# Windowed attention on one core: row scores in one block over four banks, row and column scores of a group in one step

## The reference, cut to what matters

```python
xs = jnp.roll(_gn(x), (-3, -3), axis=(-2, -1))
qkv = jnp.einsum('bchw,oc->bohw', xs, w_qkv) + b_qkv[None, :, None, None]
# -> q, k, v of shape (B, Hn, Wn, HEADS, 49, 16), 16 x 16 windows in an image
scores = jnp.einsum('bxyhqd,bxyhkd->bxyhqk', q, k) / np.sqrt(16)
out = jnp.einsum('bxyhqk,bxyhkd->bxyhqd', jax.nn.softmax(scores, axis=-1), v)
return x + roll_back(out)
```

## Time and profile before

| | |
|---|---|
| median of 3 runs | 966.29 us |
| profiled execution, whole | 967.17 us |
| profiled execution, span on the core | 965.3 us |
| PE busy | 897.0 us (93%), 46595 matmuls |
| PE weight loads busy | 724.3 us (75%) |
| DVE busy | 738.2 us (76%) |
| ACT busy | 656.9 us (68%) |
| POOL busy | 597.7 us (62%) |
| TensorE clock granted, mean | 0.986 of 2.4 GHz |
| HBM traffic | 53 GB/s |

### The profile page before, as it was taken

The page is one execution under the profiler, slowest core; times in us unless marked ns, Lnnn a source line. Parts: engine busy times, 40 slices in busy tenths (PEclk is TensorE's granted clock), DMA queues, the critical chain, the costliest instruction groups (busy, mean ns, idle before and its releaser), DMA issues.

```text
span 965.3 us, 104413 instructions
## 1 busy us (share of the span) xinstructions
PE 897.0 (93%) x46595; PEld 724.3 (75%) x46595; DVE 738.2 (76%) x1404; ACT 656.9 (68%) x1297; POOL 597.7 (62%) x1067
## 2 busy tenths in 40 slices
PE   0479999999999999999999999999999999999984
PEld 0258888887788888888778888888778888888863
DVE  6667787877878787878878787878877777777762
ACT  1346777776677777777677777777677777777752
POOL 1335666666566767676576767676666767676741
PEclk9999999999999999999999999999999999999996
DMA  9401112112112211221121000000000000000011
GB/s 372 170 4 51 50 67 67 51 49 67 51 49 67 67 53 47 67 67 54 46 67 50 17 33 33 33 17 33 34 17 33 33 33 17 33 33 33 17 36 37
DMA packets 29920, 51.96 MB, mean 54 GB/s; under 512 B 3650, under 2 KB 28868, under 8 KB 29764
## 3 DMA queue, kind: packets, MB, share of 16 engines
q1 hardware_dynamic: 29892, 51.59, 15.1%
HBM read 25.89 MB, written 25.69 MB: 53 GB/s over the span
## 4 chain that ended last, share of the span: by engine, by line
PE 86%; DVE 8%; issue 4%; POOL 1%; ACT 1%; DMA 0%; POOLq 0%; SPq 0%; DVEq 0%; ACTq 0%
PE psum L733 16%; PE psum L785 12%; PE psum L753 11%; PE psum L771 10%; PE psum L717 8%; PE psum L705 8%; PE psum L698 7%; PE psum L797 4%; PE psum L760 3%; PE psum L713 3%; PE psum L740 2%; DVE neg_max L574 2%; DVE stats L494 2%; DVE q_halves L559 1%; DVE mixed L599 1%
## 5 line engine op out<-in xcount | busy, mean ns | idle before, releaser
L374 ACT ACTIVATE probs_t<-psum,exp_scale 128x800 f32<-128x800 f32 x256 | 223.6, 925 | 177.8 <-PE psum L760 177.8
L574 DVE TENSOR_REDUCE neg_max<-psum 100x16 f32<-100x784 f32 x256 | 249.5, 974 | 43.1 <-PE psum L733 18.3
L293 POOL TENSOR_SCALAR neg_halves<-neg_max 100x32 bf16<-100x32 f32 x128 | 60.5, 473 | 289.9 <-DVE neg_max L574 289.9
L733 PEld LDWEIGHTS psum<-k_hi,q_masks 32*128 32x128 f16 x8192 | 174.7, 91 | 47.6 <-issue 46.4
L733 PE MATMUL psum<-k_hi,q_masks 32*128 32x49 f16 x8192 | 197.4, 179 | 4.5 <-issue 2.7
L733 PE MATMUL psum<-k_lo,q_masks 32*128 32x49 f16 x4096 | 182.2, 179 | 0.0
L733 PEld LDWEIGHTS psum<-k_lo,q_masks 32*128 32x128 f16 x4096 | 160.5, 91 | 0.0
L306 POOL TENSOR_TENSOR stage<-mixed,image 128x343 f32 (+7 forms) x256 | 144.7, 586 | 10.7 <-DVE mixed L599 7.2
L351 ACT ACTIVATE xn<-image,shift_c,rstd_c 128x21 f32 (+6 forms) x256 | 132.5, 575 | 8.0 <-DVE shift_c L554 6.1
L753 PE MATMUL psum<-q_masks,k_hi 32*64 32x100 f16 x8192 | 129.1, 219 | 6.1 <-issue 3.5
L785 PE MATMUL psum<-probs_t,v_rows 64*32 64x100 f32 x8192 | 132.1, 254 | 1.7 <-issue 1.7
(11 more groups left out here) (120 smaller groups left out, 1867.8 us busy)
## 6 DMA issues: line engine op xcount, KB each, us to landing
out_dram<-stage SPq DMA_DIRECT2D x64, 224.0 KB, 2.1
out_dram<-stage SPq DMA_DIRECT2D x64, 168.0 KB, 1.9
image<-in_x_dram SPq DMA_DIRECT2D x32, 224.0 KB, 2.6
image<-in_x_dram SPq DMA_DIRECT2D x1, 6104.0 KB, 27.6
image<-in_x_dram SPq DMA_DIRECT2D x34, 168.0 KB, 2.5
image<-in_x_dram SPq DMA_DIRECT2D x6, 896.0 KB, 9.8
image<-in_x_dram SPq DMA_DIRECT2D x1, 728.0 KB, 14.5
w_nat<-in_L_conv_w_qkv_dram SPq DMA_DIRECT2D x1, 192.0 KB, 2.5
```

The source lines that it names most:

```text
L374: nc.scalar.activation(probs_t[:, 2 * u:2 * u + 2, :, :].rearrange("p h a q -> p h (a q)"), psum[:, COL_BANKS[u], 0:PAIRS * ROWS2], ACT.Ex ...
L574: nc.vector.tensor_reduce(neg_max[:, par, 2 * j:2 * j + 2, :], psum[0:ROWS2, ROW_BANKS, 0:GT] .rearrange("p h (w k) -> p h w k", k=TOK), A ...
L733: last = nc.tensor.matmul(psum[:, ROW_BANKS.start + h - 2 * j, w * TOK:(w + 1) * TOK], q_masks[rows, par, low + w * ROWS2:low + w * ROWS2 ...
```

## The change

The four banks 0 to 3 hold the row scores of a group at once (`ROW_BANKS` is now two pairs), and `row_scores` is one block of 96 matmuls in which four matmuls with four different row groups follow each other. Banks 2 and 3 are also the first half of the column scores (`COL_BANKS[0]`, so that `exp(g, 0)` reads them), so the block waits for `exp(g-1, 0)`. The sums of the keys move from bank 3 to a spare part of the bank of Q and K. Row scores, turned maxima and column scores of a group all stand in one step; weighing and sums follow one step later, the projections stand one step earlier. PE's order in a step becomes: row scores of g, weighing of g-1, sums of g-1, V of g+1, turned maxima of g, Q of g+2, column scores of g, inverse of g-1, K of g+2. DVE does both maxima one after the other and has them behind `mask_q` and `scale_rows`; ACT takes the steps in a new order with both pieces of `exp` last, as before. Scale and shift of the image exist twice, so that the next image's can be written early; the statistics begin and end one pair of steps earlier. POOL's and SyncE's programs are unchanged.

```diff
-        ROW_BANKS, COL_BANKS, OUT_BANKS = slice(0, 2), (slice(6, 8), slice(2, 4)), slice(6, 8)
-        NEG_BANK, SUM_BANK, QK_BANK, V_BANK, INV_BANK = 0, 3, 4, 5, 5
+        ROW_BANKS, COL_BANKS, OUT_BANKS = (slice(0, 2), slice(2, 4)), (slice(2, 4), slice(6, 8)), slice(6, 8)
+        NEG_BANK, QK_BANK, V_BANK, INV_BANK = 0, 4, 5, 5
...
             def exp(g, u):
                 act.wait_ge(col_mm, g + 1)
-                wait(act, out_mm, g)
+                wait(act, sum_mm, g)
...
-            def step(g, n, par):
+            def step(g, n, par, b=0):                       # ACT
+                if live(g + 1):
+                    evac_k(g + 1)
+                if live(g - 1):
+                    evac_even(g - 1)
+                if live(g + 3):
+                    normalise(g + 3, n + 1 + par, 1 - par, b)
+                if live(g - 1):
+                    high_inverse(g - 1)
+                if live(g + 1):
+                    evac_v(g + 1, 1 - par)
                 if live(g):
-                    evac_k(g)
+                    evac_neg(g)
                 if live(g + 2):
-                    normalise(g + 2, n + 1, par)
-                if live(g - 2):
-                    high_inverse(g - 2)
-                if live(g - 1):
-                    evac_neg(g - 1)
-                if live(g - 2):
-                    evac_even(g - 2)
+                    evac_q(g + 2)
                 if live(g):
-                    evac_v(g, par)
-                if live(g + 1):
-                    evac_q(g + 1)
-                if live(g - 1):
-                    exp(g - 1, 0)
-                    exp(g - 1, 1)
+                    exp(g, 0)
+                    exp(g, 1)
...
                 if first:                                    # DVE
                     first()
+                if live(g + 1):
+                    mask_q(g + 1, 1 - par)
+                if live(g - 2):
+                    scale_rows(g - 2, par)
                 if live(g):
-                    mask_q(g, par)
-                if live(g - 2):
-                    invert(g - 2)
-                    low_inverse(g - 2)
+                    maximum(g, par, 0)
+                    maximum(g, par, 1)
+                if live(g - 1):
+                    invert(g - 1)
+                    join(g - 1)
+                    low_inverse(g - 1)
                 for chunk in chunks:
                     take_stats(image_at + chunk * STAT, chunk)
-                if live(g - 2):
-                    join(g - 2)
                 if before:
                     before()
-                if live(g):
-                    maximum(g, par, 0)
-                if live(g + 1):
-                    low_q(g + 1)
-                if live(g - 2):
-                    scale_rows(g - 2, par)
+                if live(g + 2):
+                    low_q(g + 2)
                 if after:
                     after()
-                if live(g):
-                    maximum(g, par, 1)
...
-            def row_scores(g, par, j):
-
-                if j == 0:
-                    pe.wait_ge(q_masked, g + 1)
-                    pe.wait_ge(k_split, g + 1)
-                    wait(pe, neg_ready, g)
-                wait(pe, max_done[1 - j], g + j)
+            def row_scores(g, par):
+                pe.wait_ge(q_masked, g + 1)
+                pe.wait_ge(k_split, g + 1)
+                wait(pe, max_done[0], g)
+                wait(pe, neg_ready, g)
+                wait(pe, exp_done[0], g)
                 for w in range(GW):
                     for n, (low, k) in enumerate(((0, k_hi), (0, k_lo), (Q_LEN, k_hi))):
-                        for h in (2 * j, 2 * j + 1):
+                        for h in range(HP):
...
             def column_scores(g, par):
-                wait(pe, exp_done[1], g)
-                wait(pe, inv_done, g)
+                pe.wait_ge(max_done[1], g + 1)
                 wait(pe, join_done, g + 1)
...
             def sum_keys(g):
-                pe.wait_ge(exp_done[0], g + 1)
-                pe.wait_ge(exp_done[1], g + 1)
+                pe.wait_ge(k_evac, min(g + 3, GROUPS) if isinstance(g, int) else g + 3)
...
             def weigh(g, par):
                 pe.wait_ge(v_evac, g + 1)
-                wait(pe, join_done, g + 1)
+                pe.wait_ge(exp_done[0], g + 1)
+                pe.wait_ge(exp_done[1], g + 1)
...
             def step(g, par):                                # PE
 
                 if live(g):
-                    project_v(g, par)
-                if live(g - 2):
-                    sum_keys(g - 2)
+                    row_scores(g, par)
                 if live(g - 1):
-                    turn_max(g - 1)
-                if live(g - 2):
-                    weigh(g - 2, par)
+                    weigh(g - 1, 1 - par)
+                    sum_keys(g - 1)
                 if live(g + 1):
-                    project_q(g + 1, 1 - par)
+                    project_v(g + 1, 1 - par)
                 if live(g):
-                    row_scores(g, par, 0)
-                if live(g - 2):
-                    spread_inverse(g - 2, live(g))
+                    turn_max(g)
+                if live(g + 2):
+                    project_q(g + 2, par)
+                if live(g):
+                    column_scores(g, par)
                 if live(g - 1):
-                    column_scores(g - 1, 1 - par)
-                if live(g):
-                    row_scores(g, par, 1)
-                if live(g + 1):
-                    project_k(g + 1, 1 - par)
+                    spread_inverse(g - 1, live(g + 1))
+                if live(g + 2):
+                    project_k(g + 2, par)
```

More of the change, by code:

```diff
@@ L125, in window_attention @@
         q_high, q_low, q_masked = sem("q_high"), sem("q_low"), sem("q_masked")
-        row_mm = [sem("row_mm_0"), sem("row_mm_1")]
+        row_mm = sem("row_mm")
         max_done = [sem("max_done_0"), sem("max_done_1")]
@@ L346, in _, with normalise @@
                                      scale=slot_of[:, w:w + 1]).then_inc(picks_made, 1)
-            def normalise(g, t, half):
+            def normalise(g, t, half, b):
                 wait(act, x_split, g)
@@ L351, in normalise @@
                     last = nc.scalar.activation(token_view(xn, piece), pixel_view(image[:, bass.ds(at, BAND)], piece),
-                                                ACT.Identity, bias=shift_c[:, 0:1], scale=rstd_c[:, 0:1])
+                                                ACT.Identity, bias=shift_c[:, b % 2:b % 2 + 1], scale=rstd_c[:, b % 2, 0:1])
                 last.then_inc(xn_ready, 1)
@@ L391, in evac_even @@
                 nc.scalar.activation(even_out[:, :, :, :], even, ACT.Identity, scale=v_scale[:, 0:1]).then_inc(even_done, 1)
-            def step(g, n, par):
+            def step(g, n, par, b=0):
[9 more added lines that the diff above has]
+                    evac_v(g + 1, 1 - par)
                 if live(g):
-                    evac_k(g)
+                    evac_neg(g)
                 if live(g + 2):
-                    normalise(g + 2, n + 1, par)
-                if live(g - 2):
-                    high_inverse(g - 2)
-                if live(g - 1):
-                    evac_neg(g - 1)
-                if live(g - 2):
-                    evac_even(g - 2)
-                if live(g):
-                    evac_v(g, par)
-                if live(g + 1):
-                    evac_q(g + 1)
-                if live(g - 1):
-                    exp(g - 1, 0)
-                    exp(g - 1, 1)
+                    evac_q(g + 2)
+                if live(g):
+                    exp(g, 0)
+                    exp(g, 1)
             act.wait_ge(norm_ready, 1)
-            step(-2, -1, 0)
+            step(-3, -2, 1)
             act.wait_ge(scales_ready, 1)
-            for g in range(-1, 4):
+            for g in range(-2, 3):
                 step(g, g // 2, g & 1)
             with act.Fori(2, BANDS - 1) as n:
+                step(2 * n - 1, n - 1, 1)
                 step(2 * n, n, 0)
-                step(2 * n + 1, n, 1)
             for b in range(1, B):
@@ L422, in _ @@
                 with act.Fori(b * BANDS - 1, (b + 1) * BANDS - 1) as n:
-                    step(2 * n, n, 0)
-                    step(2 * n + 1, n, 1)
-            for g in range(GROUPS - 2, GROUPS + 2):
+                    step(2 * n - 1, n - 1, 1, b)
+                    step(2 * n, n, 0, b)
+            for g in range(GROUPS - 3, GROUPS + 1):
                 step(g, g // 2, g & 1)
@@ L547, in scatter_groups @@
                 nc.vector.transpose(mean_c[:, :], mean_row[:, :])
-                link(nc.vector.transpose(rstd_c[:, :], var_row[:, :]))
+                link(nc.vector.transpose(rstd_c[:, b % 2, :], var_row[:, :]))
             def offer(b):
-                wait(dve, xn_ready, b * 2 * BANDS)
-                scatter_groups()
```

(57 more changed lines are left out.)

10 lines of the change are left out of this document (5 added, 5 removed).

## The result

The changed kernel takes 978.93 us (median of 4 runs, 977.27 to 979.53) where the kernel before takes 967.75 (median of 4, 965.54 to 969.62): a ratio of 1.0117, 95% interval 1.0099 to 1.0136. It is slower by 1.2%, and 940 was forecast. The time lies above the stated range.

The account below looks back on a forecast made before the run. PE's program bounds the kernel at 6.88 us a step; afterwards a four-engine circle of 6.64 would. 122 intervals save 29.3, image changes add 3: span 965.3 becomes 939.0, plus 1.9 less 0.9 gives 940.0 us, range 918 to 975.

Parts of the forecast that it names:

- The circle: Closed way from one group's column scores to the next's, over `exp`, row scores, maxima, `split_max`, turned maximum, Q: 6.64 us.
- Row scores fed at about 8 ns a matmul: PE's new block of 96 matmuls runs at the column scores' rate: 0.78 us from first to last start.
- `split_max` free of L567: On POOL, without blocking by `mask_q` on DVE, `split_max` takes 0.74 us instead of 1.09; L293 at 0.22.
- The maxima: Two maxima in a row on DVE, 0.89 and 0.97 us.
- the blocking: DVE and POOL share a port; `mask_q` moves into the stretch of `add_image` and `split_x`; DVE's margin was 0.1 to 0.6.
- rival 4: In front of DVE's maxima: `mask_q` loses to POOL's `split_x`, step 7.09 us, 55 more, 995 us; chance 0.10.
- The change of image: DVE's extra work stands between `low_q` and `mask_q`: 1 us added for each of three changes, bounds 0 and 3.
- the hops: Passages between engines on the circle, mostly taken at 0.05 us each, 0.04 from row scores to DVE.
- turned maximum 0.06: PE's turned maximum between `split_max` and Q takes 0.06 us, as a matmul of 100 columns.
- PE's own way through the circle: `weigh`, sums and V last until 4.6, `turn_max` gets its input at 4.68: nearly even.
- Rival 3: On POOL: `split_max` stays at 1.09 because something else on DVE blocks it; circle 6.99, 43 more, 983 us; chance 0.06.
- the step staying at 6.88: PE's neighbours cost a few tenths more at each of its two waits: 969 us, no change; chance 0.07.

Follow-up runs that it names:

- e6: Changed kernel with four of the five waits of `row_scores` moved before `project_k`, only `exp_done[0]` staying: 967.88 us, ratio 1.0004 to the kernel before.
- e3: Changed kernel with the three waits of `project_q` issued before `turn_max` instead of behind it: 972.62 us, ratio 1.005 to the kernel before.
- e4: Changed kernel with `project_q(g + 2, par)` before `turn_max(g)`: 947.08 us, ratio 0.9791 to the kernel before.
- e7: Changed kernel with e4 and e6 together, and `weigh` with one wait in place of three: 932.64 us, ratio 0.9631 to the kernel before.
- e5: Changed kernel with row scores back in two blocks of 48, only the second waiting for `exp` 0: 961.74 us, ratio 0.9932 to the kernel before.

## Why the prediction was wrong

**What was right.** The circle and its members, block by block. Row scores fed at about 8 ns a matmul: 0.75 where I said 0.78 (a later row of the same block stands at 566.95, the first at 566.23). `split_max` free of L567: L293 at 0.22. The maxima: 1.85 for the pair, 1.86 forecast. DVE in time in spite of the blocking: it waited 0.52 to 0.71 for the row scores, so rival 4 did not come about, though one instruction of `mask_q` rose from 427 to 498 ns in the mean. The change of image: the turned maxima from 227.8 to 259.8 take 32.0 for four steps, 4.2 more than four mean steps of 6.95; before it was 3.4, so 0.8 is new, 1 forecast.

**The step that failed** is the sum of the new circle: 6.64, and inside it the hops, which I took at 0.05 each ("to PE: 0.05, as the other hops") and "turned maximum 0.06". Measured:

| term | forecast | measured |
|---|---|---|
| `exp` to the first row score | 0.05 | 0.14 |
| last row score to the maxima | 0.04 | 0.09 |
| turned maximum to Q | 0.06 | 0.20 |
| `split_max` | 0.74 | 0.74 and 0.89 in turn |
| row scores, Q and the rest | | -0.05 together |
| circle | 6.64 | 6.87 and 7.03 |

So +0.09 + 0.05 + 0.14 = 0.28 in every step, less 0.05, and 0.15 more in every second one. The forecast gain was 0.24 a step. The sum has fourteen terms; their mechanism held, and the three hops that were off were all too short. e6 shows the first term's nature (four waits moved, 0.14 becomes 0.05, 11 us), e3 the third's: both were read where an engine had no other wait to go through. The second, 0.05 to DVE, was not tried. The 0.15 of POOL adds 0.07 a step in the mean; the prediction had one value, 0.74, and both places it was read from start L293 0.19 behind the maxima (502.79 to 502.98, 250.75 to 250.94), the early kind.

Over the run: the mean step is 0.07 longer, some 110 steps, 8 us; three changes of image 3 us; about 1 us is left for filling and draining. That is the span's 965.3 to 977.1.

**The way beside it.** The prediction called PE's and POOL's arrival at `turn_max` "nearly even", and so they are: its blocks give 6.56 for PE's own way through the circle against 6.64, and the short step shows 6.83 against 6.87. PE's way has the same two hops too short (0.09 and 0.14), and 0.06 more from the row scores to `weigh` (566.23 to 567.18, 0.95 where 0.89 was forecast). So nothing taken from one way alone helps much: e4 took 0.60 out of POOL's way and got 0.27.

**The rivals.** None named what came. Rival 3 has the nearest figure, 983, and the place: `split_max` took 0.89 in every second step; but its cause, another blocking by DVE, is not there (L293 at 0.22). The one that came nearest in kind, the step staying at 6.88 because PE's neighbours cost a few tenths more at its waits, had the right place and 0.07 of chance, and was priced at 969. The bounds were at fault too: each hop had one value and no upper end, though 0.14 in front of PE after `exp` stood in the chain of the kernel before, in its last steps, where `sum_keys` has two waits:

```profile
945.51 0.93 ACT probs_t L374
946.44 0.14 issue
```

## What to carry to other kernels

Before two stages of one item are put into the same step, write down the closed way from one item to the next with every hop on it; here PE's program was to get 0.48 us a step shorter, and a circle of four engines took its place. A hop is not one number: read it in front of a block with as many waits as the new one will have. On such a circle move work off it, not only out of the program (Q in front of the turned maximum), and let the late semaphore stand alone in front of its block.

A block that is made denser gains nothing while it must wait for what its looser form does not need: in the order of this change two loose blocks beat one dense one by 17 us, because half the work fits where PE would wait. That does not make the loose form the better one. e6 gets 11 us with the dense block by moving waits alone, e7 gets 46. In e7 only some 0.06 a step is left to fill in front of the row scores, and two blocks take 0.34 longer than one (1.28 against 0.94), so there I expect the dense block to be ahead; that is an estimate, and no run put two blocks into e7.

## What the runs showed of the hardware

- PE's start behind the semaphore it waits for last: 0.05 us where that wait stood alone before the block (L739 after POOL, L734 after `exp` in e6), 0.14 to 0.15 where it stood among several in the program (L732 after `exp`, L743 in e3), the others long met.
- Behind a block that PE had to wait for, the next block is late too if it has waits of its own: Q 0.20 after the turned maximum with three waits, 0.04 without (e3). Where PE did not have to wait for POOL (every second step of e5), Q with its three waits followed in 0.05.
- POOL's L293 starts 0.18 or 0.34 after the maxima in turn, from one step of the loop's pair to the other. In the late steps the sequencer's L290, L141 and L292 run between the two, in the early ones at most L292 is left; why the steps differ is open.
